# The first stage's PSUM bank opened by its first full product, and the four border products moved behind the third full one

## The reference

```python
Af = A_grid[None] * f[:, None]
Bf = B_grid[None] * f[:, None]
gradv_Af = _grad(Af[:, 0], 1) + _grad(Af[:, 1], 2)
gradvv_Bf = _grad2(Bf[:, 0], 1) + _grad2(Bf[:, 1], 2) + _grad(_grad(Bf[:, 2], 2), 1) + _grad(_grad(Bf[:, 2], 1), 2)
df = -gradv_Af + gradvv_Bf * 0.5
f_new = f + df * dt[:, None, None]
return jnp.maximum(f_new, 0.0)
```

## Time and profile before

| | |
|---|---|
| time of three runs | 973.41, 976.05, 976.03 us; median 976.03 |
| profiled execution, first to last instruction | 975.5 us |
| PE busy, share of the span | 90% |
| PE weight loads, DVE, ACT, POOL | 68%, 79%, 75%, 25% |
| blocks of the first stage (line 1192) | 16, started from 22.5 to 809.2 us |
| granted TensorE clock, mean | 0.78 up to 156.4 us, 1.00 after |

### The profile page before, as it was taken

How to read it: one execution, slowest core, us unless ns; L and a number is a source line. 1 busy time by engine, 2 the same in 40 slices (tenths; PEclk the granted TensorE clock), 3 DMA queues, 4 the chain that set the end, 5 groups by cost and what they waited for, 6 DMA issues and landing times.

```text
span 975.5 us, 18086 instructions
## 1 busy us (share of the span) xinstructions
PE 874.9 (90%) x5643; PEld 666.6 (68%) x5731; DVE 766.6 (79%) x2375; ACT 733.7 (75%) x1901; POOL 239.2 (25%) x237
## 2 busy tenths in 40 slices
PE   7675878998999989998999989998999989999988
PEld 6354555776777767776777767776777767767766
DVE  7467687888888888888887888888888888867532
ACT  3133777978789787978789787978789787978772
POOL 1133122222242223222232223222232223121000
PEclk9577888999999999999999999999999999999999
DMA  9815453543537254543537254544537254554500
GB/s 257 230 45 126 129 157 115 153 134 113 158 114 200 82 144 138 148 129 118 153 120 195 82 150 132 148 129 121 150 122 193 82 151 131 139 139 144 167 9 22
DMA packets 133081, 130.88 MB, mean 134 GB/s; under 512 B 18265, under 2 KB 123481, under 8 KB 132969
## 3 DMA queue, kind: packets, MB, share of 16 engines
q1 hardware_dynamic: 101072, 111.49, 40.2%
q10 hardware_dynamic: 31914, 18.23, 6.5%
HBM read 112.61 MB, written 17.07 MB: 133 GB/s over the span
## 4 chain that ended last, share of the span: by engine, by line
PE 53%; ACT 18%; DVE 17%; issue 8%; DMA 2%; POOL 2%; SPq 0%; ACTq 0%; DVEq 0%; POOLq 0%
PE ff_ps L1319 11%; PE PT_ps L1345 6%; ACT Pr L1042 5%; PE G L1115 4%; PE ff_ps L1300 4%; PE ctx_ps L1366 4%; PE scores_ps L1331 4%; PE G L1200 3%; ACT L1042 3%; DVE bias L904 3%; PE G L1123 3%; ACT tanh L1024 3%; ACT ffT L1028 2%; PE ff_ps L1286 2%; PE scores_ps L1328 2%
## 5 line engine op out<-in xcount | busy, mean ns | idle before, releaser
L1042 ACT ACTIVATE Pr<-bias,nmax 128x256 f32<-128x256 f32 x512 | 255.6, 505 | 57.9 <-DVE nmax L904 57.4
L904 DVE CUSTOM_DVE_ANT_0 bias<-scores_ps,bias 128x256 f32<-128x256 f32 x512 | 196.2, 420 | 83.9 <-issue 40.2
L1054 ACT ACTIVATE PT<-PT_ps 128x512 f32<-128x512 f32 x256 | 152.0, 594 | 65.6 <-PE PT_ps L1345 37.4
L1345 PE MATMUL PT_ps<-ident,Pr 128*128 128x128 f32 x1024 | 156.4, 275 | 9.7 <-ACT Pr L1042 9.5
L544 POOL TENSOR_TENSOR rstd<-var,half_neg 128x2 f32<-128x2 f32 (+1 forms) x64 | 40.5, 632 | 401.0 <-DVE var L669 244.6
L1345 PEld LDWEIGHTS PT_ps<-ident,Pr 128*128 128x128 f32 x1024 | 120.9, 141 | 17.5 <-ACT Pr L1042 13.8
L1300 PE MATMUL ff_ps<-ctxT,w 128*128 128x256 f32 x480 | 116.4, 385 | 16.1 <-ACT ffT L1028 15.8
L1319 PE MATMUL ff_ps<-w,ffT 128*128 128x256 f32 x480 | 114.3, 384 | 2.8 <-DVE ffT L883 2.8
L1300 PEld LDWEIGHTS ff_ps<-ctxT,w 128*128 128x128 f32 x480 | 86.4, 190 | 34.1 <-ACT ffT L1028 21.3
L1331 PE MATMUL scores_ps<-k_stack,q_stack 96*128 96x256 bf16 x512 | 99.4, 275 | 10.4 <-issue 3.4
L1042 ACT ACTIVATION_READ_ACCUMULATOR Pr<-bias,nmax 128x1 f32 x512 | 100.1, 195 | 0.0
(11 more groups left out here) (219 smaller groups left out, 1685.2 us busy)
## 6 DMA issues: line engine op xcount, KB each, us to landing
bias<-in_fside_Bx16xSxS_dram SPq DMA_DIRECT2D x256, 256.0 KB, 3.1
part_dram<-front ACTq DMA_DIRECT2D x32, 384.0 KB, 2.8
q_stack<-part_dram SPq DMA_DIRECT2D x32, 192.0 KB, 3.4
k_stack<-part_dram SPq DMA_DIRECT2D x32, 192.0 KB, 4.0
F<-in_x_dram SPq DMA_DIRECT2D x16, 256.0 KB, 3.8
ada<-rows_dram SPq DMA_DIRECT2D x16, 256.0 KB, 5.0
q_stack<-part_dram SPq DMA_DIRECT2D x32, 128.0 KB, 3.4
k_stack<-part_dram SPq DMA_DIRECT2D x32, 128.0 KB, 3.8
```

The lines of the kernel that those rows point to most:

```text
L904: nc.vector.tensor_tensor_reduce(out=t, in0=SP_[:, n % 2, q * S:(q + 1) * S], in1=t, scale=-1.0, scalar=BIG, op0=ALU.add, op1=ALU.min, acc ...
L1042: ins = nc.scalar.activation(Pr[:, n % PR, q, :], bias[:, n // CH % RING, 2 * (n % CH) + q, :], ACT.Exp, bias=nmax[:, n, q:q + 1], scale=-1.0,
L1054: nc.scalar.activation(PT[:, m % BATCH, :, :].rearrange("p c q -> p (c q)"), TP[:, m % 2, :], ACT.Identity).then_inc(pt_ok, 1)
L1345: ins = pe.transpose(TP[:, m % 2, c * S + q * P:c * S + (q + 1) * P], Pr[:, m % PR, q, c * P:(c + 1) * P], ident[:, :])
```

## The change

The product of zeros goes, with its tile and its memset, and const_set is waited for at 5 in place of 6. In the block, three full products come first, the first of them with start=True: gradT and lapT of half 0, then gradT of half 1. Then the four border products follow, in their old order, and last lapT of half 1, which raises l0_mm. The same numbers are added, in another order.

```diff
-        zeros = sb("zeros", [1, P], BF16)
...
-            nc.gpsimd.memset(zeros[:, :], 0.0).then_inc(const_set, 1)
...
-            pool.wait_ge(const_set, 6)
+            pool.wait_ge(const_set, 5)
...
-                    pe.matmul(GF[b], zeros[:, :], bc(zeros[:, :], 2 * S // P), start=True, stop=False)
+                    for m, mat, x in ((0, gradT, X1), (0, lapT, p_b0), (1, gradT, X1)):
+                        pe.matmul(GF[b][:, m, :], mat[:, m, m * P:(m + 1) * P], x[b][:, m, :],
+                                  start=(m == 0 and mat is gradT), stop=False)
                     for mat, x in ((gradT, X1), (lapT, p_b0)):
                         for m in range(2):
                             near, far = (slice(P - HALO, P), slice(0, HALO))[::1 - 2 * m]
                             pe.matmul(GF[b][near, m, :], mat[far, 1 - m, m * P + near.start:m * P + near.stop],
                                       x[b][far, 1 - m, :], start=False, stop=False)
-                    for m in range(2):
-                        for mat, x in ((gradT, X1), (lapT, p_b0)):
-                            ins = pe.matmul(GF[b][:, m, :], mat[:, m, m * P:(m + 1) * P], x[b][:, m, :],
-                                            start=False, stop=(m == 1 and mat is lapT))
-                    ins.then_inc(l0_mm, 1)
+                    pe.matmul(GF[b][:, 1, :], lapT[:, 1, P:2 * P], p_b0[b][:, 1, :],
+                              start=False, stop=True).then_inc(l0_mm, 1)
```

More of the change, by code:

```diff
@@ L934, in _ @@
                 nc.vector.memset(upT[t * A:(t + 1) * A, 1 - t, :], 0.0).then_inc(up_zero, 1)
-            dve.wait_ge(const_set, 6)
+            dve.wait_ge(const_set, 5)
             run(dve, head, front, back)
@@ L1143, in front @@
                 if once("s_h2t", j, n):
-                    pe.wait_ge(const_set, 6)
+                    pe.wait_ge(const_set, 5)
                     pe.wait_ge(h2_raw_ok, 1)
```

## The result

| | median | lowest to highest | runs |
|---|---|---|---|
| before | 976.03 us | 972.97 to 978.21 | 9 |
| after | 969.56 us | 964.73 to 971.42 | 9 |

The ratio is 0.9936, 95% interval 0.9917 to 0.9954: the change takes 6.5 us off by the medians (6.2 by the ratio). The forecast was 971.4 us and the range began at 969.8, so the direction was right and the measured time lies 0.24 us under the range.

A forecast was written before the change was run, and what follows sets the result against it. PE was taken to bound the kernel; 3.84 us (twelve later blocks) plus 0.75 (early blocks) made 4.6 off the 975.5 us span, 970.9, and with 0.5 for the median 971.4 us. The 8-in-10 range was 969.8 to 975.2 us.

The forecast's parts named there:

- What bounds the kernel: PE, busy 90% of the span; the chain of waits passes through 15 of the 16 blocks, twelve at full clock.
- What one block costs: Block on PE at full clock: 3.44 us before, 3.12 after, 0.32 saved: 0.22 the zeros instruction, 0.10 one shape change.
- the bounds of 0.22 and 0.38: Limits for the unseen step from fp32 full into fp32 border, taken as 0.31 us; 0.25 to 0.41 saved a block.
- Full drain at a change of shape: Skill's rule read literally: next product starts 0.38 us after the one ahead; 0.38 saved a block, 4.6 us for twelve.
- Absorbed: Rival: PE time goes, but the chain moves to DVE and ACT, giving back half or more: 973.1 to 976.3, chance 0.17.
- Not what it says: Rival: leading full products' weight loads can't run ahead behind the wait on l0_in; 2.1 us saved, 973.9, chance 0.08.
- The twelve later blocks: Blocks behind 156.4 us, at full clock: 0.32 us saved each, 3.8 us in all (3.0 to 4.9).
- The early blocks: First four blocks, where PE waits: 0.25 us saved at the lower clock level in three, 0 in one: 0.75 us.
- How the numbers follow: Chances from the cases: faster 0.71, same 0.24, slower 0.05; forecast case 970.4 to 972.6 us at 0.62.
- the bound of 4.9 us on the later blocks: Upper end of the saving counted for the twelve blocks at full clock, 3.0 to 4.9 us around 3.8.
- More than counted: Rival: whole printed duration at each shape change, or early blocks pulling waits along; 6.9 us saved, 969.1 to 970.3, chance 0.07.
- Slower, by the clock: Rival: in the first 156 us PE waits more, adding 1.2 GHz stretches; 981.4 with 20 us more, chance 0.06.

The follow-up runs named there:

- e2: Kernel before with the new block in the twelve later blocks only, first four as before: 971.34 us, ratio 0.9945.
- e3: The changed kernel timed once more, no edit, beside runs of the kernel before: 969.99 us, ratio 0.9944.
- e4: Kernel before with the row of zeros made a full 128 x 128 tile, same ten products in the same order: 974.26 us, one run.
- e5: The new product order with the product of zeros kept to open the bank, against the kernel before: 978.31 us, one run.
- e7: New block everywhere, but tile of zeros, memset and wait for six constants kept as in the kernel before: 966.52 us, ratio 0.9919.
- e9: Kernel before, old block, with 30 more filler products in the first pair's stages: 972.83 us, ratio 0.9976.
- e6: Changed kernel with 30 more filler products in the first pair's stages, where PE stands idle: 964.13 us, ratio 0.9904 to the kernel before.
- e10: Changed kernel with the same 30 more filler products, a second set of runs: 965.91 us, ratio 0.9912 to the kernel before.
- e1: Kernel before with the new block in the first four blocks only, twelve later as before: 972.47 us, ratio 0.9982.
- e8: Kernel before with 54 filler products at the start in place of 50: 975.19 us, ratio 0.9992.

## Why the prediction missed its range

Point by point, by its own steps:

- **What bounds the kernel: right.** The chain still passes through the blocks, and the later stretch is shorter by all that PE saves: 762.1 us against 758.3 in e2 and e3. From the fifth block to the fifteenth, a steady turn is 0.66 us shorter in e3 than before, where 0.64 had been named as the sign.
- **What one block costs: right.** 3.12 us, with the unseen step from fp32 full into fp32 border at 0.31, as taken; the bounds of 0.22 and 0.38 weren't needed. e4 splits the 0.32 into 0.22 and 0.10, as the sum had it, and e5 shows the same prices added up the other way.
- **Full drain at a change of shape: not seen.** The step from fp32 full into fp32 border is 0.31 us. The Trainium skill (TensorEngine Tiling (Array Packing), Tiling Modes, Key Properties) says that changing the mode drains TensorE; a wait for the printed end of the MATMUL ahead would have put it at 0.38. That end is modelled, so the rows speak against a wait until then and not against every drain; the measured price of a change is 0.10 us.
- **Absorbed: did not happen.** The hand-over at 0.38 us stayed at 0.38. That PE's weight loads were busy only 68% of the time, which had spoken for this rival, did not mean slack: all twelve later blocks paid in full. **Not what it says: did not happen**; the weights of the leading full product run ahead behind the wait.
- **The twelve later blocks: 3.84 us counted, 3.80 measured.** In the profile after alone it is 3.3; that execution's turns were some 0.08 us longer than those of the same kernel in e3, for which no run here gives a reason.
- **The early blocks: the steps were right, their clock was taken as given.** I had counted them as if the clock met them as in the one profile: 0.75 us. The rows above show 0.23 us for a block at the lower level and 0.11 at the upper, and at equal clock the four gave 1.05 ± 0.35, in which 0.75 lies. But what a set of runs shows is this and 0.28 us for each us of difference at the lower level, with a standard deviation of 5 to 9 us from run to run, that is some 2 us. With that included the four gave 1.5 ± 0.6.
- **How the numbers follow: here is the step that failed.** I let the clock act in one direction only (the rival that made the kernel slower) and gave the median of before an error of "up to about 1 us" from three runs that spread over 2.6 us. The single runs of before cover 9.5 us, and the median of 61 of them is 975.31, 0.7 below the one I started from. A comparison of nine runs with nine carries an interval of about 1.8 us either way by itself. The range's low end should have been the counted 971.4 less that, 969.6, and less again for the bound of 4.9 us on the later blocks. With it, 969.56 would have been inside. So the step that failed is the clock's term: downward it stood at nothing, and the spread of a median at 1 us. The change is worth 4.85 us at equal clock; the remaining 1.6 us of the first comparison lie within its interval. That it was only scatter is not shown: over all sets the change gave 6.0 ± 0.5 us. The later sets show that the clock scatters single times by that much; for the nine runs of before in that first comparison the clocks are not on record, so that it was the clock there too is inferred, not shown.
- **More than counted: the case that came, for a cause that it did not name.** The later blocks show neither a longer step nor waits pulled along; what goes beyond the count is in the first stretch, where the clock is the likely cause. The case was also priced wrongly: a wait of 0.38 us at each change of shape makes 4.6 us for the twelve blocks, and the 4.9 that it used is the opposite bound, a step into the border without any extra.
- **Slower, by the clock: the sensitivity was well taken (0.5 us for each us while PE is in the chain; 0.28 on average), the sign was not.**
- I set the median 0.5 us above the profile's span. The time of a run lies 1.8 us above its span in the runs of before (2.0 for the changed kernel; 1.8 for e7, which keeps the memset, so 0.2 us of the 7.7 us between the two spans is not in the times). So the profile shown was of a run of some 977.3 us, at the slow end, with 68 us at the lower level where 61 is the mean. The forecast was a difference and did not suffer, but it should have told me that one profile's first stretch is not the average one.

**What stays open:** whether the new block leaves the clock at its upper level more of the time, which would make the 6.0 us its true worth, or whether that excess over 4.85 is chance. Without fillers the early blocks' share is -1.1 ± 1.7 us at the lower level, worth 0.3 us; with fillers the pair e9 and e6/e10 suggests 7 us, worth 2. Why e7 gained more than expected. And why e9 gains less from fillers than the changed kernel.

**A version that beats both:** the changed kernel with the 30 fillers of e6, 964.1 and 965.9 us in two sets of six runs. That is 10 to 11 us under the kernel before by medians, 7.5 to 9.3 by means, since one run in six stays slow. It was never run beside the changed kernel itself: the medians of separate sets are 5 us apart, e7, the new block beside e6, was 2.4 us above it, and the fit gives the fillers 2.2 ± 0.6 us in all.

## What to carry to other kernels

Price a block of products by start-to-start distances, with changes of the array's shape as an item of their own: group products of one shape, and let an accumulation be opened by a product that is needed anyway. If the chain of waits passes through the block and the next engine had been waiting for longer than is saved, the count comes out to a few hundredths of a microsecond for each block. But where a kernel has a stretch in which TensorE waits often and its clock changes level, read the run-to-run spread of that stretch before giving a range, and compare kernels behind it, or at equal clock.

## What the runs showed of the hardware

- A change of shape costs 0.10 us on top of the 0.216 us step, in every pairing seen: fp32 128 x 128 to bf16 1 x 128, to fp32 32 x 32 and back, bf16 1 x 128 to fp32 32 x 32 and to fp32 128 x 128, bf16 128 x 128 to fp32 32 x 32. The step into the border took no longer although those products add to places that the full ones ahead have just written.
- Behind a change of shape into fp32 128 x 128 the second MATMUL comes 0.32 us after the first (804.03 to 804.35 above).
- The later stretch repeats closely from execution to execution: 761.9 to 762.2 us in four profiles with the old block (before, e1, e8, e9), 758.1 to 758.4 in six with the new one and 758.8 in a seventh. The first stretch of the changed kernel varied by 4.1 us between two profiles, with fillers by 10.4.
- An early block of the old kind took 5.95 us at the lower clock level and 3.12 at the upper one, the same instructions in the third block of e2 and of e8.
